# Moving the down products of each routed expert unit into the unit that follows, and loads and splits with them

## The reference, cut to what matters

```python
x = x + xattn(layernorm(x), ctx_1024, ...)       # 512 queries, 8192 keys
x = x + attn(layernorm(x), ...)                  # causal, 512 rows
x = x + ffn(layernorm(x), ...)
# ffn:
scores = softmax(x_flat @ gate_w.T)              # 8 experts, the best 2 of each row
gu = einsum('nh,eih->nei', x_flat, experts_gate_up)
h = silu(gu[..., :704]) * gu[..., 704:]
expert_out = einsum('nei,ehi->neh', h, experts_down)
out = einsum('neh,ne->nh', expert_out, w)        # w: scores of the best 2, else 0
shared = silu(x_flat @ shared_gate_w.T) * (x_flat @ shared_up_w.T) @ shared_down_w.T
out = out + sigmoid(x_flat @ shared_expert_gate_w.T) * shared
```

## Time and profile before

| What | Value |
|---|---|
| median of 3 runs | 686.71 us (685.3 to 690.03) |
| profiled execution, its own time | 686.13 us |
| its span, first to last instruction | 684.4 us |
| granted TensorE clock | 1.000, on average |
| PE busy | 678.1 us, 99% of the span |
| PEld, DVE, ACT, POOL busy | 82%, 81%, 50%, 31% |
| units 0 to 10 on PE | 515.76 to 655.08 us of the span |
| what 16 DMA engines moved in the span | 134.33 MB, 196 GB/s on average |

### The profile page before, as it was taken

The page is one execution under the profiler, slowest core; times in us unless marked ns, Lnnn a source line. Parts: engine busy times, 40 slices in busy tenths (PEclk is TensorE's granted clock), DMA queues, the critical chain, the costliest instruction groups (busy, mean ns, idle before and its releaser), DMA issues.

```text
span 684.4 us, 9739 instructions
## 1 busy us (share of the span) xinstructions
PE 678.1 (99%) x3156; PEld 562.4 (82%) x3156; DVE 553.8 (81%) x722; ACT 340.3 (50%) x460; POOL 211.4 (31%) x167
## 2 busy tenths in 40 slices
PE   8999999999999999999999999999999999999997
PEld 7788888888888788888888888888888888888886
DVE  6588898777979998899998662669658998998937
ACT  5522222222245565566665342652356888888830
POOL 4754445445440000000000000225762433434360
PEclk9999999999999999999999999999999999999999
DMA  8467767767742236422320330713267999999723
GB/s 288 190 202 230 227 219 234 252 221 229 256 148 93 93 118 250 186 92 92 101 83 0 155 139 0 307 47 112 106 203 271 338 363 369 382 377 394 269 91 124
DMA packets 41742, 134.33 MB, mean 196 GB/s; under 512 B 6576, under 2 KB 13104, under 8 KB 38384
## 3 DMA queue, kind: packets, MB, share of 16 engines
q1 hardware_dynamic: 39184, 127.39, 52.8%
q0 software_dynamic: 1520, 5.05, 1.9%
q10 hardware_dynamic: 1008, 1.51, 0.7%
HBM read 123.78 MB, written 10.15 MB: 196 GB/s over the span
## 4 chain that ended last, share of the span: by engine, by line
PE 94%; DVE 2%; DMA 2%; ACT 1%; issue 1%; DVEq 0%; ACTq 0%; SPq 0%
PE ps L1075 26%; PE ps L1017 9%; PE ps L1018 8%; PE ps L1021 8%; PE ps L1313 5%; PE ps L912 4%; PE ps L914 4%; PE ps L913 4%; PE ps L1270 4%; PE ps L1294 3%; PE ps L1292 3%; PE ps L1293 3%; PE ps L982 2%; PE ps L929 2%; DMA raw_u<-up_in 1%; PE ps L1202 1%
## 5 line engine op out<-in xcount | busy, mean ns | idle before, releaser
L492 POOL TENSOR_TENSOR c_lo<-ring,c_hi 128x512 fp32r<-128x512 f32 x64 | 87.0, 1362 | 86.0 <-ACT c_hi L639 86.0
L639 ACT ACTIVATE c_hi<-ring 128x512 fp32r<-128x512 f32 x64 | 40.5, 633 | 128.5 <-PE ps L1021 86.0
L509 POOL TENSOR_TENSOR w_lo<-raw,w_hi 128x1024 fp32r<-128x1024 f32 x11 | 27.5, 2497 | 248.2 <-ACT w_hi L762 236.0
L1017 PE MATMUL ps<-qk_hi,c_hi 128*128 128x512 f32 x256 | 99.9, 390 | 0.0
L1018 PE MATMUL ps<-qk_lo,c_hi 128*128 128x512 f32 x256 | 99.6, 389 | 0.0
L1509 DVE TENSOR_TENSOR runmax<-runmax,att 128x512 f32<-128x512 f32 x64 | 83.9, 1311 | 3.7
L1503 DVE SCALAR_TENSOR_TENSOR att<-ring,beta,ps 128x512 f32 (+1 forms) x64 | 47.8, 746 | 26.6 <-PE ps L1021 25.6
L1021 PE MATMUL ps<-qk_hi,c_lo 128*128 128x512 f32 x256 | 68.6, 389 | 0.0
L1075 PE MATMUL ps<-p_hi,d_hi 128*128 128x512 f32 x256 | 63.8, 391 | 0.0
L1075 PE MATMUL ps<-p_hi,d_lo 128*128 128x512 f32 x256 | 63.3, 389 | 0.0
L1075 PE MATMUL ps<-p_lo,d_hi 128*128 128x512 f32 x256 | 63.2, 389 | 0.0
(11 more groups left out here) (320 smaller groups left out, 1466.9 us busy)
## 6 DMA issues: line engine op xcount, KB each, us to landing
ring<-stream SPq DMA_DIRECT2D x64, 512.0 KB, 4.3
raw_u<-up_in SPq DMA_DIRECT2D x22, 1024.0 KB, 7.0
raw_d<-down_in SPq DMA_DIRECT2D x33, 512.0 KB, 7.7
ring<-ctx_in SPq DMA_DIRECT2D x32, 512.0 KB, 3.3
raw<-shared_in SPq DMA_DIRECT2D x11, 768.0 KB, 5.8
raw_u<-up_last_in SPq DMA_DIRECT2D x11, 768.0 KB, 7.8
slots<-blank SPq DMA_DIRECT2D x15, 264.0 KB, 5.1
late<-wqkv_in SPq DMA_DIRECT2D x1, 3072.0 KB, 10.6
```

The source lines that it names most:

```text
L492: pool.tensor_tensor(c_lo[:, s % 2, :], ring1[:, s, 0, :], c_hi[:, s % 2, :].bitcast(F32), ALU.subtract).then_inc(lo1_ready, 1)
L639: act.activation(c_hi[:, s % 2, :], ring1[:, s, 0, :], ACT.Copy).then_inc(hi1_ready, 1)
L1017: pe.matmul(ps[:, s, :], hi, qk_hi[:, k, :], start=(k == 0), stop=False)
```

## The change: what it does

The three down products of unit u now stand in unit u + 1, one behind each of its up products. In PE's list of a unit u the order is now: up 0; turning of the hidden chunk 2 of unit u - 1; down 0 of unit u - 1; up 1; turnings of hidden chunk 0 and of the next unit's rows; up 2; down 1 of u - 1; turning of hidden chunk 1; down 2 of u - 1. Behind the last unit its turning of chunk 2 and its three down products follow, between the two sides of the shared chunk 8. The third up chunk gets PSUM bank 7 (`up_bank`), and PE's wait for `prod_e_done` at the head of the unit, which guarded bank 0, is gone.

The splits move along. ACT makes `wd_hi` of chunks 1 and 2 of unit u - 1 at the head of unit u, and `wu_hi` of the next unit's chunk 1 now ahead of `silu_e(u, 2)` and `gathered_high`. DVE makes the second half of chunk 1 and the whole of chunk 2 of `wu_lo` at the head of the unit that uses them, and `wu_lo` of chunk 0 in one instruction and not in two halves. POOL's `down_last_low(u)` waits for the low parts of all three up chunks of unit u + 1 (3u + 6 and not 3u + 4). SP issues the loads of the down weights half a unit or more later. The number of bytes, matmuls and splits is the same.

```diff
         ps = scope.enter_context(nc.psum_tensor("ps", [P, 8, 512], F32))
+
+        up_bank = (0, 1, 7)
...
                     load_rows(u)
                 load_up(u, expert_, 0)
                 if not second:
-                    load_down(u - 1, expert_before, 2)
+                    load_down(u - 1, expert_before, 0)
                 load_up(u, expert_, 1)
                 if second:
                     sp.wait_ge(down_done, LEAD - 1 + CREDIT)
                     for early in range(2, AHEAD_ROWS):
                         load_first_rows(early)
                 load_up(u, expert_, 2)
-                load_down(u, expert_, 0)
-                load_down(u, expert_, 1)
+                if not second:
+                    load_down(u - 1, expert_before, 1)
+                    load_down(u - 1, expert_before, 2)
...
                     load_unit(E + m, sp.value_load(which[0:1, m:m + 1], min_val=0, max_val=E - 1), before_)
-            load_down(extra + (E - 1), sp.value_load(last_expert[0:1, 0:1], min_val=0, max_val=E - 1), 2)
+            expert_last = sp.value_load(last_expert[0:1, 0:1], min_val=0, max_val=E - 1)
+            for c in range(CH):
+                load_down(extra + (E - 1), expert_last, c)
...
             def down_last_low(u, last=False):
                 pool.wait_ge(dn_hi_ready, u * CH + CH)
                 if not last:
-                    pool.wait_ge(up_lo_ready, u * CH + (CH + 1))
+                    pool.wait_ge(up_lo_ready, u * CH + 2 * CH)
...
-            def unit(u, first=False, second=False, last=False):
+            def unit(u, units_before=2, first_kept=False, last=False):
+                if units_before == 2:
+                    keep(u - 2, first=first_kept)
+                if units_before:
+                    down_high(u - 1, 1)
+                    down_high(u - 1, 2)
                 silu_e(u, 0)
-                down_high(u, 1)
-                if not first:
-                    keep(u - 1, first=second)
+                if units_before:
+                    hidden_high(u - 1, 2)
                 if not last:
                     up_high(u + 1, 0)
-                else:
+                if units_before:
+                    act.wait_ge(y_psum_e, u * CH + (1 - CH))
+                down_high(u, 0)
+                if last:
                     shared_sides_high(LEAD + 1)
                     shared_down_high(LEAD + 1)
                 silu_e(u, 1)
                 hidden_high(u, 0)
-                if not first:
-                    act.wait_ge(y_psum_e, u * CH)
-                down_high(u, 2)
+                if not last:
+                    up_high(u + 1, 1)
                 silu_e(u, 2)
+                if not last:
+                    gathered_high(u + 1)
                 hidden_high(u, 1)
                 if not last:
-                    gathered_high(u + 1)
-                    up_high(u + 1, 1)
-                    hidden_high(u, 2)
                     up_high(u + 1, 2)
-                    act.wait_ge(y_psum_e, u * CH + 1)
-                    down_high(u + 1, 0)
-                else:
...
+            gathered_high(0, bank=gate_bank(LEAD - 2))
             act.wait_ge(rows_out, 16 * 2 * ST)
-            down_high(0, 0)
-            gathered_high(0, bank=gate_bank(LEAD - 2))
-            unit(0, first=True)
-            unit(1, second=True)
+            unit(0, units_before=0)
+            unit(1, units_before=1)
+            unit(2, first_kept=True)
             final = act.value_load(more[0:1, 0:1], min_val=0, max_val=MORE) + (E - 1)
-            with act.Fori(2, final) as e:
+            with act.Fori(3, final) as e:
                 unit(e)
             unit(final, last=True)
+            keep(final - 1)
+            down_high(final, 1)
+            down_high(final, 2)
+            hidden_high(final, 2)
...
-            def unit(u, first=False, last=False, ahead=False):
-                if not first:
-                    pe.wait_ge(prod_e_done, u * CH)
+            def unit(u, units_before=2, last=False, ahead=False):
                 up(u, 0)
-                if not first:
-                    down(u - 1, 2)
-                if first:
-                    pe.wait_ge(added, 1)
+                if units_before:
+                    turn_hidden(u - 1, 2)
+                    if units_before == 2:
+                        pe.wait_ge(y_ready, u - 1)
+                    down(u - 1, 0)
+                up(u, 1)
+                turn_hidden(u, 0)
+                if not units_before:
+                    pe.wait_ge(added, ST)
                 if not last:
                     turn_gathered(u + 1, ahead=ahead)
-                if first:
-                    pe.wait_ge(added, ST)
-                up(u, 1)
-                turn_hidden(u, 0)
                 up(u, 2)
+                if units_before:
+                    down(u - 1, 1)
                 turn_hidden(u, 1)
-                if not first:
-                    pe.wait_ge(y_ready, u)
-                down(u, 0)
-                turn_hidden(u, 2)
-                down(u, 1)
+                if units_before:
+                    down(u - 1, 2)
...
-            unit(0, first=True, ahead=True)
-            for u in range(1, AHEAD_ROWS - 1):
-                unit(u, ahead=True)
+            for u in range(AHEAD_ROWS - 1):
+                unit(u, units_before=min(u, 2), ahead=True)
...
             wait_split(LEAD)
             side_shared(LEAD, 0, gate_bank(LEAD), g_psum)
-            down(final, 2)
+            turn_hidden(final, 2)
+            pe.wait_ge(y_ready, final)
+            for c in range(CH):
+                down(final, c)
             side_shared(LEAD, 1, 2 + gate_bank(LEAD), u_psum)
...
@@ -1907,25 +1917,24 @@
                     dve.wait_ge(down_done, LEAD + CREDIT)
                     for st in (2, 0, 1, 3):
                         add_shared(st)
+                else:
+                    up_low_half(u, 1, True)
+                    up_low(u, 2)
                 product_e(u, 0)
-                down_low(u, 1)
+                if not first:
+                    hidden_low(u - 1, 2)
+                    down_low(u - 1, 1)
                 if not last:
-                    up_low_half(u + 1, 0, False)
+                    up_low(u + 1, 0)
                 product_e(u, 1)
                 hidden_low(u, 0)
+                down_low(u, 0)
+                product_e(u, 2)
                 if not last:
-                    up_low_half(u + 1, 0, True)
-                product_e(u, 2)
+                    gathered_low(u + 1)
                 hidden_low(u, 1)
                 if not last:
-                    gathered_low(u + 1)
                     up_low_half(u + 1, 1, False)
-                    hidden_low(u, 2)
-                    up_low_half(u + 1, 1, True)
-                    up_low(u + 1, 2)
-                    down_low(u + 1, 0)
-                else:
-                    hidden_low(u, 2)
...
             up_low(0, 2)
-            down_low(0, 0)
             unit(0, first=True)
             final = dve.value_load(more[0:1, 0:1], min_val=0, max_val=MORE) + (E - 1)
             with dve.Fori(1, final) as e:
                 unit(e)
             unit(final, last=True)
+            down_low(final, 1)
+            hidden_low(final, 2)
```

7 lines of the change are left out of this document (3 added, 4 removed).

## The result

Before, the median is 688.25 us over six runs (685.3 to 690.03), after it is 698.95 us (697.83 to 701.3). The ratio is 1.0167, with a 95% interval of 1.0137 to 1.0196: the change makes the kernel slower by 1.7%, some 11 us. The forecast was 690.3, and its range ended at 695.2.

The account below looks back on a forecast made before the run. PE, busy 99% of the span, was taken as the bound, with DVE setting the pace after the change; 2.0 (start) + 1.2 (units) + 0.4 (end) = 3.6 us more gave 690.3 us, range 685.6 to 695.2.

Parts of the forecast that it names:

- Part 1: PE's order in a unit: one return from transposes to matmuls fewer, 0.12 us saved, 12.56 us a unit at full pace.
- Part 2: Start: unit 0 loses 3.08 us of down products, unit 1 starts about 1.1 us earlier; cost 2.0 us, bounds 0 and 3.1.
- Part 3: Routed units: DVE stands 1.3 us behind POOL's subtraction and sets the pace at 13.0 us; +1.2 us over nine units.
- my upper bound of 2.27: DVE's stand behind POOL's subtraction in each unit if the short rows cover nothing, making the unit 13.8 us.
- another starting point of POOL's row: Sign that the sum is wrong as a whole: POOL's subtraction starts elsewhere than behind chunk 2's split.
- 0.2 for the rest: DVE's unit: 0.2 us added for what the store's small rows and waits for ACT leave of the old stretch.
- Part 4: Down chunk loads in the units: issued later, each with half a unit of room as before, hidden, so no cost.
- rival B: Units: the load of up chunk 1 sets the pace at 13.5 us, +8.1 us in sum, 694.8 us; chance 0.18.
- both of the signs that I had named for it: In the units: ACT idle for `raw_u` ahead of chunk 1 in most units, and windows over 13.3 us.
- The ring worked out for it: Up chunk 1's buffer, round: 7.4 us landing, then ACT's and DVE's rows, 13.7 less 0.2 overlap, 13.5 us.
- Part 5: End, behind the last unit: the last store comes 1 to 2 us later against PE; cost 0 to 2, taken as 0.4.
- Rival A: Units: DVE isn't held, PE sets the pace at 12.56 us; sum -0.3 us, 686.4 us; chance 0.22.

Follow-up runs that it names:

- e1: Changed kernel with POOL's subtraction of down chunk 2 cut to one column and loads of down chunks 0 and 1 halved from unit 1: 687.99 us, ratio 1.0009.
- d3: Kernel before, with POOL's subtraction of down chunk 2 cut to one column of 512 in each half tile from unit 1 on: 686.14 us, ratio 0.9982.
- c1_warm: Changed kernel with seven 128x128 matmuls of ones filling PE's gap ahead of unit 1: 697.63 us, ratio 1.0149.
- a2: Changed kernel with ACT's split of the next unit's up chunk 1 put back behind the copy of the turned rows: 696.19 us, ratio 1.0133.
- c2_dve: Changed kernel with the subtraction of down chunk 2 (units 0 to 9) moved from POOL to DVE, behind that of down chunk 1: 693.55 us, ratio 1.0092.
- d4_twice: Changed kernel with POOL's subtraction of down chunk 2 made twice, one behind the other: 714.0 us, ratio 1.038.
- c4: Changed kernel with the loads of down chunks 0 and 1 cut to half of their bytes from unit 1 on: 694.71 us, ratio 1.0102.
- e2: Kernel before, with the loads of down chunks 0 and 1 cut to half of their bytes from unit 1 on: 685.33 us, ratio 0.9976.
- a1: Changed kernel with POOL's subtraction of down chunk 2 cut to one column of each row of 512 from unit 1 on: 691.51 us, ratio 1.0066.
- a3: Changed kernel with POOL's subtraction cut to one column and ACT's split of up chunk 1 put back behind the turned rows' copy: 690.32 us, ratio 1.0053.
- d2: Kernel before, with down chunk 2's subtraction on DVE, right behind the low part of the turned rows, where DVE waits for ACT: 686.92 us, ratio 0.9995.
- c3: Kernel before, with down chunk 2's subtraction moved from POOL to DVE, between its rows of up chunks 1 and 2: 700.12 us, ratio 1.0201.
- d1: Changed kernel with down chunk 2's subtraction on DVE, ACT's up chunk 1 split put back, and matmuls of ones in PE's gap: 691.38 us, ratio 1.0057.

## Why the prediction was wrong

It said 3.6 us more; the medians rose by 10.7 and the profiled executions by 12.9.

**Part 1, PE's order: near in the number, not in the reason.** Freed of DVE's blocks and of late loads a unit takes 12.59 to 12.62 (e1), where 12.56 was worked out. But the old order reaches the same 12.59 to 12.62 once POOL's row is cut (d3), with its four returns from transposes. So no run shows a gain from the new order of PE. The return that is saved is paid back beside it: in unit 5 the turnings that now stand together take 0.57 us from the first of them to the next product (e1), where the same two took 0.35 and 0.14 (d3). And what a quick unit of the kernel before takes above 12.60, its 12.67, goes with POOL's row there and not with the returns.

**Part 2, unit 0: right in its sum, and blind to what follows.** Unit 0 took 10.35 for a forecast 10.3, and PE stood 1.77 us for a forecast 1.9. That the matmuls behind such a gap mostly run at about half the clock was not in the sum. c1_warm, which fills the gap and changes nothing else, puts it at 1.26 us in the profile's unit 1. The executions of e1 with and without the fall lie 1.1 us apart. In the changed kernel itself, where DVE and loads set the pace behind it, the 1.2 us between the medians are not beyond their intervals.

**Part 3, DVE against POOL: the mechanism right, the term mis-sized.** I wrote that DVE stands "2.40 - 0.13 - 1.0 = 1.3 us in each unit". It stood 1.76: 1.48 in four units, 2.33 in four, 0.61 in one. The step that failed is that POOL's subtraction starts with DVE's split of up chunk 2. In half of the units POOL was late, because its store took 2.35 us beside a DVE row and not 1.02, and then the three short rows cover nothing, which was my upper bound of 2.27. The prediction had named another starting point of POOL's row as a sign that its sum is wrong. I had read the block in one direction only. In DVE's account this is 9 x 0.46 = 4.1 us of the excess. Where POOL was on time and no load in the way, the unit came out as forecast: a2's units of that kind took 13.0, though with 1.48 of block where I had 1.3 and 0.2 for the rest. c2_dve and d4_twice show the mechanism from both sides: without POOL's row 0.75% faster although DVE has more to do, with two of them 2.1% slower.

**Part 4, the loads: wrong.** "They are hidden in the forecast", and with units longer than before "late loads have some slack", I wrote. They got none: a buffer's next load is issued when DVE has split the one before, and ACT needs up chunk 1 ahead of its third silu. DVE idled 0.54 us a unit where I had put 0.2 for this and the rest, 3.1 us over nine units; some 1.5 of them lie in unit 1 beside the slow clock. The experiments give the loads 0.65% in the changed kernel by the bytes (c4) and 0.34% by the place on ACT (a2). The two are different ways to take away one wait and are not to be added. This is rival B's mechanism, and both of the signs that I had named for it came: ACT idle for `raw_u` in most units, and windows over 13.3. The ring worked out for it was right to 0.1 us, and it set the pace in units 3, 5, 7 and 9. The slack that I counted on isn't there, because the length of that ring doesn't contain DVE's block: the load is issued at the head of a unit and needed in the same unit. It did not set the pace alone: even with ACT's place undone the kernel stood at 1.0133.

**Part 5, the end: about right.** 3.67 - 3.08 = 0.6 us against 0.4. Start, clock and end together can be read from the profiles of the two runs with the light loads. They reach unit 10 at the same time (642.03 and 642.05 us), and from there e1 takes 44.5 us and e2 41.5. The medians are 0.0033 apart, 2.3 us, but e1 has POOL's row cut as well, which was worth up to 0.18% in the kernel before.

**Shares.** From 1.0167, POOL's row cut is worth 1.01%, the bytes 0.65%, and both 1.58%, nearly the sum. What stays, 0.09%, is the moved start, the clock and the end, less what the same two cuts bring in the kernel before (0.18% and 0.24%). Rival A's time, no slower than before, was nearly reached by this cut kernel (e1), and by no other form of the change. Both causes came mostly with the new order: the same cuts are worth 0.18% and 0.24% in the kernel before. My range left both out because I gave each bound its own place, 13.8 us as the end of part 3 and 13.5 as rival B, and took neither as likely with the other. In the kernel the two take turns, unit by unit, and each unit is as long as the longer of the two rings makes it.

What stays open: why the clock did not fall in a1 and a3, and what makes the blocks of 1.48 and 2.33 us take turns. Late loads aren't needed for it, as a2 keeps the turns almost without them, but no run moved the store alone. The 0.42 us by which the units begin later say nothing: in the profiled executions of the old order they begin at 515.74 to 516.52, and of the new at 515.55 to 517.66.

## What to carry to other kernels

When two engines shut each other out of a port, draw both queues over one period: what the slower engine issues ahead of the disputed row can itself be held, and then the cover that you counted on has already passed. An engine at 90% of the pace has no slack to give. POOL's subtraction cost at most 0.3% while it hid in DVE's idle stretch, and 1.0% when it was moved beside full rows. The same row made by DVE cost nothing in that stretch and 2% on the path (d2 and c3). And where a load is issued and needed in the same unit, a longer unit doesn't buy it any time. Work out the ring of the load beside the ring of the engine: when both are near the pace, their turns make the units longer on average than either alone.

## What the runs showed of the hardware that was not expected

- POOL's issue of an indirect store took 1.02 us before, where it began beside a DVE row of 0.42 us that reads PSUM, and 2.35 or 1.82 beside DVE rows with two SBUF operands. That fits what was left of that row, and 1.02 behind it. That the issue itself waits is worked out from these starts and ends, not shown by an experiment.
- PE idle for 1.77 us ahead of unit 1 (busy 8.58 of unit 0's 10.35 us) was followed by 4 us at a granted clock of 0.57 to 0.60 in six of eight profiled executions and of 1.00 in two; with matmuls of ones in the gap it was 1.00 in both (c1, d1). The fall cost 1.1 us between e1's executions with and without it. What separates the six from the two stays open.
- A POOL subtraction of two numbers a partition took 1.12 us on average, 1.23 to 1.25 where it met DVE's down split and 0.19 where it didn't (a1): cutting an instruction's size doesn't take its place in the turns away.
- Taking some 11% of the bytes off the queues (0.5 of 4.5 MB a unit) shortened the median landing of the up chunks from 7.4 us (a1) to 5.8 (e1). In c4's profiled execution, the slowest of its four, the same cut left it at 7.3, so the shorter landing didn't come with the bytes alone.
